# Dense first stage of a two-layer graph network: GpSimd centres one of a block's four tiles, and converts gather indices two steps at once

## What is computed

```python
h = jnp.maximum(_layernorm(x, axis=-1), 0.0)
x = x + _L0_gnn_ref(h, src, dst, W1, b1, W2, b2)      # two layers
# a layer: concatenate([h, mean of h[src] by dst, mean of h[dst] by src]) @ W + b
```

```python
h = jnp.maximum(_layernorm(x, axis=-1), 0.0)
x = x + _L1_gnn_ref(h, edge_index, edge_attr_64, u, batch0, w1, b1, w2, b2, w3, b3)
```

## Time and profile before

| | us |
|---|---|
| median of 3 runs | 4395.07 |
| lowest and highest | 4391.62, 4395.31 |
| the profiled execution | 4389.29 |
| its span | 4387.3 |
| the dense stage in it | from about 17 to about 524 |

### The profile page before, as it was taken

One profiled execution on the slowest core, in us unless ns is written; L12 is line 12 of the kernel. 1 busy time (PEld: TensorE's weight loads), 2 busy tenths in 40 slices (PEclk: granted clock), 3 DMA queues, 4 the chain that ended last, 5 costly groups with the idle time before them and its releaser, 6 DMA issues.

```text
span 4387.3 us, 96510 instructions
## 1 busy us (share of the span) xinstructions
PE 3723.6 (85%) x24424; PEld 3208.4 (73%) x24424; DVE 3176.7 (72%) x10907; ACT 2195.5 (50%) x5395; POOL 3210.1 (73%) x3158
## 2 busy tenths in 40 slices
PE   7999887888888857677767767599999999999999
PEld 5666577777777746666666666488888888888888
DVE  8999888888888822222322222299999999999998
ACT  6777633333333322222222222277777777777776
POOL 6666568888888778888888888666666666666665
PEclk9999999999999978888888888799999999999999
DMA  7889766766666668888888888756666666666664
GB/s 231 257 249 260 223 153 155 157 153 153 155 157 157 137 154 198 205 202 197 205 202 196 204 205 196 164 126 135 134 134 134 134 134 135 134 135 134 135 134 99
DMA packets 973215, 742.15 MB, mean 169 GB/s; under 512 B 192386, under 2 KB 834890, under 8 KB 973178
## 3 DMA queue, kind: packets, MB, share of 16 engines
q1 hardware_dynamic: 731706, 574.62, 43.7%
q0 software_dynamic: 241472, 167.10, 27.8%
HBM read 431.94 MB, written 309.52 MB: 169 GB/s over the span
## 4 chain that ended last, share of the span: by engine, by line
PE 39%; DMA 11%; POOL 6%; issue 5%; DVE 2%; SPq 1%; ACT 1%; DVEq 0%; ACTq 0%; POOLq 0%
PE bank L1381 8%; DMA keyall<-keyrow 5%; PE bank L1396 4%; PE bank L1394 4%; PE bank L1395 4%; DMA ends<-pre,index 4%; POOL node L568 3%; POOL ends L553 2%; PE bank L1354 2%; PE bank L1358 2%; PE bank L1355 2%; PE bank L1356 2%; PE bank L1359 2%; DMA node<-summed,rep_index 2%; PE bank L1368 2%
## 5 line engine op out<-in xcount | busy, mean ns | idle before, releaser
L532 POOL DMA_INDIRECT pre<-summed,rep_index x392 | 620.4, 1583 | 149.9 <-issue 119.0
L568 POOL DMA_INDIRECT node<-summed,rep_index x392 | 623.3, 1590 | 131.7 <-issue 111.8
L599 POOL TENSOR_TENSOR resid<-node_out,b3s 128x128 f32<-128x128 f32 x784 | 336.8, 461 | 487.4 <-DVE rows L1119 482.5
L1031 DVE TENSOR_SCALAR same<-keyall,keys 128x512 f32<-128x512 f32 (+3 forms) x392 | 136.2, 408 | 659.8 <-DMA keyall<-keyrow 659.8
L767 ACT ACTIVATE small<-bank,bias_small 128x512 f32<-128x512 f32 x784 | 534.7, 682 | 109.2 <-PE bank L1359 62.4
L1072 DVE SCALAR_TENSOR_TENSOR z<-bank,bias,small 128x512 f32<-128x512 f32 x784 | 548.8, 740 | 13.7 <-ACT small L767 8.5
L609 POOL TENSOR_TENSOR z_lo<-z,z_hi 128x512 fp32r<-128x512 f32 x392 | 495.0, 1281 | 14.4 <-ACT z_hi L799 14.4
L722 ACT ACTIVATE endsT<-bank,b1col 128x512 f32<-128x512 f32 x98 | 67.3, 687 | 838.6 <-PE bank L1270 838.6
L553 POOL DMA_INDIRECT ends<-pre,index x392 | 382.5, 976 | 123.9 <-issue 107.9
L1179 PE MATMUL bank<-upper,table 112*128 112x256 bf16 x2744 | 338.2, 284 | 139.0 <-DVE upper L919 139.0
L1179 PEld LDWEIGHTS bank<-upper,table 112*128 112x128 bf16 x2744 | 271.3, 102 | 196.7 <-DVE upper L919 156.8
(11 more groups left out here) (143 smaller groups left out, 9810.1 us busy)
## 6 DMA issues: line engine op xcount, KB each, us to landing
node<-blank SPq DMA_DIRECT2D x98, 768.0 KB, 4.8
node_out<-node SPq DMA_DIRECT2D x196, 384.0 KB, 3.5
rows<-in_x_dram SPq DMA_DIRECT2D x196, 256.0 KB
pre<-node_out SPq DMA_DIRECT2D x196, 256.0 KB, 3.1
rows<-pre SPq DMA_DIRECT2D x196, 256.0 KB, 4.6
normed<-in_x_dram SPq DMA_DIRECT2D x196, 256.0 KB, 5.5
y<-node_out SPq DMA_DIRECT2D x196, 256.0 KB, 3.0
node_out<-y POOLq DMA_DIRECT2D x196, 256.0 KB, 4.6
```

What stands on the lines that cost most here:

```text
L532: pool.indirect_dma_start(pre1, bass.IndirectOffsetOnAxis(ap=rep_index[:, b, s:s + 1], axis=0), summed[:, b, s, 0:F], None, compute_op=ALU ...
L568: pool.indirect_dma_start(node1, bass.IndirectOffsetOnAxis(ap=rep_index[:, b, s:s + 1], axis=0), summed[:, b, s, :], None, compute_op=ALU. ...
```

## The change

VectorE centres three of the four tiles (128x384). GpSimd centres the fourth, in a new function `centre_last`, with its own semaphore `a_last`, for which TensorE's transposes and SyncE's load of the same buffer now wait as well as for `a_centred`. GpSimd's index conversion moves out of `pick` into `pick_index`, which converts the two columns of a group at once; it is called once in front of the stage and then in each second step, behind the gather, for the group ahead, when the earlier gathers from those index columns have landed. In layer one the semaphore `b_todump` is merged into `b_moved`, which now counts three per group, so that the number of semaphores stays as it was.

```diff
@@ sync: load
                     sp.wait_ge(a_centred, st.k - 3)
+                    sp.wait_ge(a_last, st.k - 3)
@@ gpsimd
+            def pick_index(first, g):
+
+                pool.tensor_copy(index[:, first:first + 2, 3:4], keys[:, 0, 0:2, bass.ds(g, 1)]).then_inc(a_index, 1)
+
             def pick(st):
 
                 b = st.b
                 if st.after(4):
 
                     pool.wait_ge(a_keep[b], 16 * (st.turn - 1))
-                    hold(pool)
-                pool.tensor_copy(index[:, b, 3:4], keys[:, 0, st.half, bass.ds(st.g, 1)]).then_inc(a_index, 1)
-                pool.wait_ge(a_index, st.k + 1)
+                pool.wait_ge(a_index, st.g + 1)
                 hold(pool)
                 pool.indirect_dma_start(picked[:, b, :], None, x,
                                         bass.IndirectOffsetOnAxis(ap=index[:, b, 3:4], axis=0)).then_inc(a_pick[b], 16)
 
+            def centre_last(st):
+
+                pool.wait_ge(a_load[st.b], 16 * st.turn)
+                pool.wait_ge(a_moments, st.k + 1)
+                if st.after(4):
+
+                    pool.wait_ge(a_T, st.k - 3)
+                pool.tensor_tensor(normed[:, st.b, T - 1, :], rows[:, st.b, T - 1, :], moments[:, st.b, T - 1, 0:1].to_broadcast([P, F]),
+                                   ALU.subtract).then_inc(a_last, 1)
+
             pool.wait_ge(s_keys, 1)
+            pick_index(0, 0)
 
             def tick(at):
                 st = at(0)
                 if st.exists:
                     pick(st)
+                    if st.half == 1 and not st.last:
+                        ahead = at(-1)
+                        if st.after(3):
+
+                            for q in (ahead.b, ahead.b + 1):
+                                pool.wait_ge(a_pick[q], 16 * (ahead.turn - 1))
+                        hold(pool)
+                        pick_index(ahead.b, ahead.g)
+                    centre_last(st)
@@ vector: tick
-                    dve.tensor_tensor(normed[:, st.b], rows[:, st.b], moments[:, st.b, :, 0:1].to_broadcast([P, T, F]),
-                                      ALU.subtract).then_inc(a_centred, 1)
+                    dve.tensor_tensor(normed[:, st.b, 0:T - 1], rows[:, st.b, 0:T - 1],
+                                      moments[:, st.b, 0:T - 1, 0:1].to_broadcast([P, T - 1, F]), ALU.subtract).then_inc(a_centred, 1)
@@ tensor: dense_transposes
                 pe.wait_ge(a_centred, st.k + 1)
+                pe.wait_ge(a_last, st.k + 1)
```

12 lines of the change are left out of this document (6 added, 6 removed).

## The result

The changed kernel takes 4376.1 us (median of six runs, 4374.0 to 4384.0), the kernel before, timed beside it, 4393.3 us (six runs, 4391.6 to 4395.3). The ratio is 0.9967 with a 95% interval of 0.9956 to 0.9977. The medians lie 17.2 us apart, 0.4%, which is more than the 0.2% that a measurement of this kernel can tell from no change. The forecast was 4372.5 us with a range of 4363 to 4416, and faster at 0.60. The forecast gain was 22.6 us; 17.2 came.

What follows compares the result with a forecast made beforehand. VectorE was taken to bound the dense first stage at 2.555 us per step; -26.5 us for the centring plus 3.9 us for the gather's writes gave -22.6 us, so 4395.07 became 4372.5 us, range 4363 to 4416.

Steps and rivals of the forecast that it cites:

- What bounds the kernel: Dense first stage: VectorE sets the pace, 2.55 us per step over 196 steps; TensorE's own pace is 2.28 us.
- -0.135 us per step for the centring: VectorE's centring shrinks from 512 to 384 elements with nothing covering it: 26.5 us gained over 196 steps.
- The subtraction is held by the centring and costs VectorE nothing: GpSimd's subtraction waits out VectorE's centring, then runs 0.46 us under the next step's statistics; VectorE loses 0.
- the first rival: GpSimd's subtraction gets in first and holds the second pair's one-hot 0.20 to 0.40 us per step: slower, chance 0.21.
- +0.02 us per step for the gather's writes: The gather's late part disturbs VectorE's one-hots by 0 to 0.11 us; 0.02 taken, 3.9 us over 196 steps.
- The two together: VectorE's loss to GpSimd's subtraction (0) plus its loss to the gather's writes (0.02 us per step): 3.9 us.
- Added waits at no cost: TensorE's transposes and SyncE's loads also wait for GpSimd's tile: shifted once or by under half a microsecond, no cost.
- Rival 2: GpSimd's step becomes 2.71 us, VectorE idles waiting for counts: +30 us, 4425 us, chance 0.05.
- Rival 4: DMA engines, limited to 92% busy, keep the first stage's step at 2.47 us: -16.7 us, 4378 us, chance 0.08.
- The end of the stage and the stages behind: Last one-hot's delay by GpSimd's blank-row fill may go: 0 to -1.5 us, counted 0; later stages keep their length.

Runs made afterwards that it cites:

- wait_centred: Changed kernel, but GpSimd's subtraction waits for VectorE's centring of the same step instead of the moments: 4389.6 us, ratio 0.9991.
- tile_left_out: Changed kernel, but nobody centres the fourth tile (TensorE transposes the third twice), GpSimd only gathers and converts: 4378.8 us, ratio 0.9960.
- two_tiles_load_first: two_tiles with the next load ahead of the store of gathered rows in SyncE's queue: 4350.7 us, ratio 0.9909.
- wait_onehots: Changed kernel, but GpSimd's subtraction also waits for the step's second one-hot pair: 4376.0 us, ratio 0.9967.
- two_tiles: wait_onehots, but GpSimd centres two of the four tiles and VectorE two: 4374.1 us, ratio 0.9964.
- centre_only: Changed kernel, but indices are converted one at a time right ahead of each gather, as before the change; GpSimd still centres the fourth tile: 4400.6 us, ratio 1.0016.
- load_first: wait_onehots with the next block's load ahead of the store of gathered rows in SyncE's queue: 4365.7 us, ratio 0.9945.
- gather_steered: Changed kernel, but the gather also waits for the step's moments and the subtraction for VectorE's centring: 4412.7 us, ratio 1.0051.

## Why the prediction was right, and where it was off

- **What bounds the kernel.** Right. VectorE set the pace. Index conversion alone changed nothing, and what the steps gained (15.2 us) and when the stage ended (14.5 us earlier) agree within 1 us.
- **-0.135 us per step for the centring.** Right: 0.610 to 0.476 from start to start, -26.3 us of the forecast 26.5. A size difference taken from another operation held to a hundredth of a microsecond.
- **The subtraction is held by the centring and costs VectorE nothing.** Right in 135 of 192 steps (1.03 us long, as the conversion of the earlier trace rows with its 0.93 had shown), wrong in 57, and this zero is the term that failed: +8.6 us on the second high one-hot where the sum has 0. In the 57 the first rival's mechanism came true. It was decided by less than 0.1 us: short ones mostly began 2.12 us after the centring, held ones 2.20, the one-hot 2.19. The rival had expected one answer for all steps, at 0.20 to 0.40 us; it was 30% of them at 0.15 to 0.19, too little to turn the sign. The prediction had the clue in its hands and used it only against the rival as a whole: in the loop's printed order the wait for the moments stands on an instruction of its own ahead of three of four subtractions. Those three are held, and the fourth is the short one (135 of 136 with that instruction held, 59 of 60 without it short). Read step by step it would have given one short subtraction in four, some 0.16 x 196 / 4 = 8 us, a price worked out afterwards from the runs. No run moved that instruction by itself, so this is a sorting without a rival in sight and not a test.
- **+0.02 us per step for the gather's writes (3.9 us).** The size is near: the first high one-hot lost 0.013 us per step, 2.5 us, most of it from the gathers that follow a short subtraction. The forecast put the gather 0.76 us behind the start of the statistics, 1.24 us behind the centring's; it stood at 0.96 behind the centring's, because the subtraction was over 0.80 us behind the centring's start and not 0.94, and the gap ahead of the gather was 0.15 us and not 0.30. Both places cost nothing, so that this miss did no harm is luck. The price for a gather in the wrong place (0.11 us, from the earlier trace rows) was of the right size, and wait_centred, tile_left_out and two_tiles_load_first paid 0.1 to 0.2 us in a sixth to two thirds of their steps.
- **The two together** were forecast at 3.9 us and measured at 11.1 (0.057 us per step). Of that error the time of the changed kernel shows only a part, 4376.1 against 4372.5 us: the steps account for 15.2 of the 17.2 us, and the kernel before came out at 4393.3 us in six runs, 1.7 us below the 4395.07 from which the forecast started.
- **Added waits at no cost.** Nearly right in the changed kernel: VectorE waits for rows under 1 us in all. But the text said that loads are issued more than a step ahead and would move by under half a microsecond; they moved by 1.07 us (5.58 to 4.51; by 0.74 in the second profiled execution). The cover was still thick enough. It was gone as soon as GpSimd became 0.1 to 0.3 us later or VectorE faster (wait_onehots, two_tiles), and it was a store behind a gather in SyncE's queue, which the text hadn't named, that stood ahead of the load.
- **Rival 2, GpSimd as the pace.** Not in the changed kernel. centre_only, slower than before by 0.16%, comes near it, with no slack left on GpSimd, but its sign (VectorE idle, waiting for counts) isn't there: VectorE is busy 451.7 of 460 us and loses by collisions.
- **Rival 4, the DMA engines.** Its bound of 2.47 us lies close to the changed kernel's 2.486, and by coincidence: load_first runs at 2.43 us with the same bytes, at 0.95 busy. A share of 0.92 was no limit.
- **The end of the stage and the stages behind.** The stage's end moved by 14.5 us, against 15.2 by the operations. Layer one gave 6 us back in the first profiled execution and none in the second; this lies within what the kernel varies by.

## What to carry to other kernels

When an instruction of one engine can hold up one of another (here GpSimd's subtraction the one-hot, or the centring the subtraction), an edit is worth what the *order of arrival* makes of it: find the instruction that decides it and release the other engine by the semaphore of the last instruction that must not be disturbed, not by the earliest that would be allowed (here the second pair of one-hots instead of the moments). Then look at what stands in the issuing queues behind the engine that was made later: a load that feeds the bottleneck shouldn't stand behind a store that waits for a slower engine. A collision removed and a time unchanged isn't proof that the collision cost nothing; wait_onehots and the load ahead of the store together gave the whole forecast, and the first alone nothing.

## What the runs showed of the hardware

- A gather on GpSimd disturbs a high one-hot on VectorE if it began about 0.52 to 0.78 us ahead of it; the one-hot then takes up to 0.50 us instead of 0.31 (tile_left_out, wait_centred). A gather that begins 0.43 to 0.50 us ahead of one (all cases in the changed kernel, wait_centred and tile_left_out), or in the centring's second half (gather_steered), costs VectorE nothing. centre_only is the exception: there one gather in four that began 0.45 us ahead held the one-hot for 0.28 us. I had expected the whole gather to be of one kind.
- A gather is itself longer when it *begins* under certain operations of VectorE: 1.33 us under a centring of four tiles, 1.09 under a high one-hot (wait_centred), 0.97 otherwise. A one-hot that it disturbs with its late part doesn't lengthen it (0.95 us in the rows of tile_left_out).
- A gather whose wait is released late begins some 0.8 us behind what released it (gather_steered, the moments), while one with nothing to wait for follows the subtraction after 0.15 to 0.4 us.
- A 128x128 subtraction takes GpSimd 0.40 us when undisturbed, a 128x256 one 0.60 to 0.64 us: the second tile costs 0.2 us, half of the first.
- The 16 DMA engines moved 274 GB/s over 460 us at a share of 0.94, 7% more than in the kernel before (255 GB/s at 0.88), without VectorE waiting for more than 3.6 us.
